# Cross-attention and LoRA experts in float32r: other operand addresses for TensorE, and context means from row sums

## The reference, cut to what matters

```
def attention(h, ctx, mask):                 # h = layernorm(x)
    scores = einsum('bsd,bmd->bsm', h, ctx) / sqrt(1024)
    attn = softmax(where(mask, scores, -1e30))
    return einsum('bsm,bmd->bsd', attn, ctx)   # 0 where nothing is valid
x = x + attention(layernorm(x), ctx, mask)
y = layernorm(x)
base = einsum('btd,od->bto', y, weight)        # 1024 x 1024
logits = einsum('btd,ed->bte', y, router_w)    # 8 experts, the best 2 are used
w_dense = top-2 of softmax(logits), normalised, else 0
Ax = einsum('nd,erd->ner', y, lora_A)          # rank 16 each, 128 columns in all
out = x + base + 2 * einsum('ner,ne,eor->no', Ax, w_dense, lora_B)
```

## Time and profile before

| | before |
|---|---|
| median of three runs | 1052.81 us |
| the profiled execution | 1052.97 us |
| its span | 1051.1 us |
| TensorE matmuls busy | 1042.2 us (99%) |
| VectorE busy | 832.1 us (79%) |
| ScalarE busy | 478.1 us (45%) |
| GpSimd busy | 143.3 us (14%) |

### The profile page before, as it was taken

The page is one execution under the profiler, slowest core; times in us unless marked ns, Lnnn a source line. Parts: engine busy times, 40 slices in busy tenths (PEclk is TensorE's granted clock), DMA queues, the critical chain, the costliest instruction groups (busy, mean ns, idle before and its releaser), DMA issues.

```text
span 1051.1 us, 18389 instructions
## 1 busy us (share of the span) xinstructions
PE 1042.2 (99%) x5849; PEld 1016.9 (97%) x5849; DVE 832.1 (79%) x2230; ACT 478.1 (45%) x930; POOL 143.3 (14%) x278
## 2 busy tenths in 40 slices
PE   7999999999999999999999999999999999999998
PEld 7999999999999999999999999999999999999998
DVE  6988887888777987878877888878888778788763
ACT  7754544445434544444444345344444444443420
POOL 3210111111111111111111111111111111111100
PEclk9999999999999999999999999999999999999999
DMA  8555555654456555575545655455654565554431
GB/s 304 198 168 131 134 153 169 164 155 115 146 160 180 143 132 127 148 200 133 153 116 148 185 150 150 135 132 168 166 151 138 120 171 153 153 149 114 114 78 55
DMA packets 156095, 156.61 MB, mean 149 GB/s; under 512 B 93968, under 2 KB 128912, under 8 KB 156048
## 3 DMA queue, kind: packets, MB, share of 16 engines
q1 hardware_dynamic: 155184, 154.63, 54.0%
q10 hardware_dynamic: 864, 1.45, 0.4%
HBM read 78.74 MB, written 33.55 MB: 107 GB/s over the span
## 4 chain that ended last, share of the span: by engine, by line
PE 96%; DVE 2%; DMA 1%; POOL 0%; issue 0%; ACT 0%; ACTq 0%; DVEq 0%; POOLq 0%
PE base_ps L1106 28%; PE base_ps L1108 28%; PE base_ps L1107 28%; PE s_ps L1133 5%; PE ro_ps L1177 3%; PE ro_ps L1178 3%; DMA xT_raw<-in_xT 1%; DVE w_lo L337 0%; DVE x_first L896 0%; DVE stats L902 0%; DVE xT_parts L815 0%; POOL w_lo L337 0%; PE h_ps L1113 0%; POOL rstd L489 0%; PE base_ps L1150 0%
## 5 line engine op out<-in xcount | busy, mean ns | idle before, releaser
L1106 PE MATMUL base_ps<-w_hi,xT_hi 128*128 128x388 f32 x1512 | 513.9, 340 | 0.0
L1108 PE MATMUL base_ps<-w_hi,xT_lo 128*128 128x388 f32 x1512 | 512.5, 339 | 0.0
L1107 PE MATMUL base_ps<-w_lo,xT_hi 128*128 128x388 f32 x1512 | 511.4, 338 | 0.0
L1107 PEld LDWEIGHTS base_ps<-w_lo,xT_hi 128*128 128x128 f32 x1512 | 284.8, 188 | 2.7
L1106 PEld LDWEIGHTS base_ps<-w_hi,xT_hi 128*128 128x128 f32 x1512 | 284.0, 188 | 2.7
L1108 PEld LDWEIGHTS base_ps<-w_hi,xT_lo 128*128 128x128 f32 x1512 | 284.3, 188 | 0.0
L493 POOL TENSOR_TENSOR rstd<-var_eps,neg_half 128x1 f32<-128x1 f32 x64 | 61.4, 959 | 571.6 <-DVE var_eps L909 571.6
L918 DVE STREAM_TRANSPOSE x2T<-xq 128x512 f32<-128x512 f32 x122 | 121.2, 1069 | 5.1 <-DMA xq<-xn 4.9
L614 ACT CAST xT_hi<-x2T 128x512 fp32r<-128x512 f32 x122 | 69.7, 618 | 79.5 <-DVE x2T L918 79.5
L933 DVE MAX8 top<-base_ps 128x8 f32<-128x8 f32 x64 | 11.1, 174 | 91.7 <-PE base_ps L1108 91.7
L608 ACT ACTIVATE xn<-w_raw,shift,rstd 128x1024 f32<-128x1024 f32 x32 | 39.9, 1246 | 96.5 <-POOL shift L496 96.5
(11 more groups left out here) (131 smaller groups left out, 1342.8 us busy)
## 6 DMA issues: line engine op xcount, KB each, us to landing
xT_raw<-in_xT SPq DMA_DIRECT2D x62, 512.0 KB, 5.3
xq<-xn SPq DMA_DIRECT2D x244, 128.0 KB, 3.6
w_raw<-in_x SPq DMA_DIRECT2D x32, 512.0 KB, 3.5
out<-x_first SPq DMA_DIRECT2D x32, 512.0 KB, 2.7
out<-w_raw SPq DMA_DIRECT2D x31, 512.0 KB, 2.7
x_first<-in_x SPq DMA_DIRECT2D x30, 512.0 KB, 3.5
h<-w_raw SPq DMA_DIRECT2D x248, 16.0 KB, 1.9
w_raw<-w_raw SPq DMA_DIRECT2D x236, 16.0 KB, 2.7
```

Of the source, the lines that this page charges most:

```text
L1106: pe.matmul(out_, a_hi, w_h, start=start, stop=False, skip_group_check=again)
L1107: pe.matmul(out_, a_hi, w_l, start=False, stop=False, skip_group_check=again)
L1108: return pe.matmul(out_, a_lo, w_h, start=False, stop=stop, skip_group_check=again)
```

## The change

The column groups become 392, 384 and 384, and the output columns 256, 384 and 384. The two groups of 384 now stand first in the row, so they begin at bytes 0 and 1536 and the group of 392 at byte 3072; the rows are padded to 1168 columns, 4672 bytes. The total of columns stays 1160. The tiles of one or a few columns are allocated last, so every operand of TensorE in the loop begins on a multiple of 64 bytes.

```
-    SIDE = WC // 6 * 2
+    SIDE = WC // 48 * 16
     W0 = O - 2 * SIDE
-    GROUPS = [(0, W0 + LR), (W0 + LR, SIDE), (W0 + LR + SIDE, SIDE)]
+    WP = -(-WC // 16) * 16
+    GROUPS = [(2 * SIDE, W0 + LR), (0, SIDE), (SIDE, SIDE)]
...
-        w_hi = sb("w_hi", [P, C, WC], f32r)
-        w_lo = sb("w_lo", [P, C, WC], f32r)
+        w_hi = sb("w_hi", [P, C, WP], f32r)
+        w_lo = sb("w_lo", [P, C, WP], f32r)
...
+        row_sums = sb("row_sums", [P, P])
...
-        any_valid = sb("any_valid", [P, 1])
```

```
+                if j == 3 and exists((b, TPB)):
+                    sp.wait_ge(row_sum_stored, b * 16 + 16)
+                    sp.dma_start(row_sums[:, :], ctx_rows.rearrange("q o -> o q").to_broadcast([P, P]))\
+                      .then_inc(row_sums_loaded, 16)
                 store(tile)
...
+                if j == TPB - 5 and exists((b, TPB)):
+                    act.wait_ge(row_sum_done, b + 1)
+                    act.dma_start(ctx_rows, row_sum[:, :]).then_inc(row_sum_stored, 16)
+                if j == TPB - 4 and exists((b, TPB)):
+                    ctxT_high(b + 1)
...
+            def ctx_row_sum(b):
+                dve.wait_ge(ctx_loaded, b * 16 + 16)
+                dve.tensor_reduce(out=row_sum[:, :], in_=ctx_raw[:, 0:D], axis=AX.X, op=ALU.add).then_inc(row_sum_done, 1)
+
             def ctx_centre(b):
-                dve.wait_ge(ctx_mean_done, b + 1)
-                dve.tensor_tensor(ctxT_centred[:, :, :], ctxT_raw[:, :, :],
+                dve.wait_ge(ctxT_loaded, b * 16 + 16)
+                dve.wait_ge(row_sums_loaded, b * 16)
+                for j in range(2):
+                    keys = ctxT_raw[:, :, j * QP:(j + 1) * QP]
+                    sums = row_sums[:, :].rearrange("p (r j) -> p j r", j=Q)[:, j]
+                    dve.scalar_tensor_tensor(out=keys, in0=sums.unsqueeze(1).to_broadcast([P, C, QP]), scalar=-1.0 / D,
+                                             in1=keys, op0=ALU.mult, op1=ALU.add).then_inc(ctx_centred, 1)
...
                 base(tile, 0, range(C))
-                if j == TPB - 4 and exists((b, TPB)):
-                    ctx_mean(b + 1)
                 base(tile, 1, range(HC))
```

More of the change, by code:

```diff
@@ L33, in xattn_lora_moe_kernel @@
     out: bass.AP,
+    ctx_rows: bass.AP,
 ):
@@ L132, in xattn_lora_moe_kernel @@
         ctxT_raw = sb("ctxT_raw", [P, C, M])
-        ctxT_centred = sb("ctxT_centred", [P, C, M])
         ctx_sum = sb("ctx_sum", [P, M])
+        row_sums = sb("row_sums", [P, P])
         mask_f = sb("mask_f", [P, M])
         mask_bias = sb("mask_bias", [P, M])
-        any_valid = sb("any_valid", [P, 1])
         x_first = sb("x_first", [P, XF, D])
@@ L152, in xattn_lora_moe_kernel @@
         one_dth = sb("one_dth", [P, P])
+        s_part = sb("s_part", [P, M])
+        s_all = sb("s_all", [P, M])
+        e_all = sb("e_all", [P, M])
+        e_split = sb("e_split", [P, 2 * M], f32r)
+        eT = sb("eT", [P, P], f32r)
+        h = sb("h", [P, ER])
+        hT_hi = sb("hT_hi", [P, P], f32r)
+        hT_lo = sb("hT_lo", [P, P], f32r)
+        row_sum = sb("row_sum", [P, 1])
+        any_valid = sb("any_valid", [P, 1])
         iota8 = sb("iota8", [P, E])
@@ L167, in xattn_lora_moe_kernel @@
         shift2 = sb("shift2", [P, 1])
-        s_part = sb("s_part", [P, M])
-        s_all = sb("s_all", [P, M])
         neg_max = sb("neg_max", [P, 1])
-        e_all = sb("e_all", [P, M])
-        e_split = sb("e_split", [P, 2 * M], f32r)
         e_sum = sb("e_sum", [P, 1])
@@ L175, in xattn_lora_moe_kernel @@
         e_scale = sb("e_scale", [P, 1])
-        eT = sb("eT", [P, P], f32r)
         top8 = sb("top8", [P, 8])
@@ L184, in xattn_lora_moe_kernel @@
         w_dense = sb("w_dense", [P, E])
-        h = sb("h", [P, ER])
-        hT_hi = sb("hT_hi", [P, P], f32r)
-        hT_lo = sb("hT_lo", [P, P], f32r)
         x_rest = [w_raw[0], w_raw[1], w_raw[1], w_raw[1]]
@@ L278, in xattn_lora_moe_kernel @@
         ctx_mean_done = sem("ctx_mean_done")
+        row_sum_done = sem("row_sum_done")
+        row_sum_stored = sem("row_sum_stored")
+        row_sums_loaded = sem("row_sums_loaded")
         ctx_centred = sem("ctx_centred")
@@ L453, in step @@
                     load_ctx(b + 1)
-                    sp.wait_ge(ctx_centred, b + 1)
+                    sp.wait_ge(ctxT_split, b + 1)
                     load_ctxT(b + 1)
@@ L532, in ctxT_high @@
             def ctxT_high(b):
-                act.wait_ge(ctx_centred, b + 1)
-                act.copy(ctxT[:, :, 0:M], ctxT_centred[:, :, :]).then_inc(ctxT_hi_done, 1)
+                act.wait_ge(ctx_centred, b * 2 + 2)
+                act.copy(ctxT[:, :, 0:M], ctxT_raw[:, :, :]).then_inc(ctxT_hi_done, 1)
             def ctx_high(b):
@@ L671, in step @@
                 gate_exp(tile)
-                if j == TPB - 4 and exists((b, TPB)):
-                    ctxT_high(b + 1)
                 if turned_on_pe(nxt2, 5):
@@ L770, in mask, with first_ctx_sum, first_ctx_centre @@
                 dve.reduce_max(any_valid[:, :], mask_f[:, :], AX.X).then_inc(mask_step, 1)
[L772 to L775, removed]
+            def first_ctx_sum():
+                dve.wait_ge(ctxT_loaded, 16)
+                dve.wait_ge(ctxT_rest_loaded, 16)
                 dve.tensor_reduce(out=ctx_sum[:, :], in_=ctxT_raw[:, :, :].rearrange("p c m -> p m c"), axis=AX.X,
                                   op=ALU.add).then_inc(ctx_sum_done, 1)
+            def ctx_row_sum(b):
+                dve.wait_ge(ctx_loaded, b * 16 + 16)
+                dve.tensor_reduce(out=row_sum[:, :], in_=ctx_raw[:, 0:D], axis=AX.X, op=ALU.add).then_inc(row_sum_done, 1)
             def ctx_centre(b):
-                dve.wait_ge(ctx_mean_done, b + 1)
-                dve.tensor_tensor(ctxT_centred[:, :, :], ctxT_raw[:, :, :],
+                dve.wait_ge(ctxT_loaded, b * 16 + 16)
[5 more added lines that the diff above has]
+                                             in1=keys, op0=ALU.mult, op1=ALU.add).then_inc(ctx_centred, 1)
+            def first_ctx_centre():
+                dve.wait_ge(ctx_mean_done, 1)
+                dve.tensor_tensor(ctxT_raw[:, :, :], ctxT_raw[:, :, :],
                                   h_ps[:, P:P + M].unsqueeze(1).to_broadcast([P, C, M]),
-                                  ALU.subtract).then_inc(ctx_centred, 1)
+                                  ALU.subtract).then_inc(ctx_centred, 2)
             def ctxT_low(b):
                 dve.wait_ge(ctxT_hi_done, b + 1)
-                dve.tensor_tensor(ctxT[:, :, M:2 * M], ctxT_centred[:, :, :], ctxT[:, :, 0:M].bitcast(f32),
+                dve.tensor_tensor(ctxT[:, :, M:2 * M], ctxT_raw[:, :, :], ctxT[:, :, 0:M].bitcast(f32),
                                   ALU.subtract).then_inc(ctxT_split, 1)
@@ L1006, in step @@
                 h_transposes(tile)
-                if j == TPB - 4 and exists((b, TPB)):
-                    ctx_centre(b + 1)
                 if j == TPB - 3 and exists((b, TPB)):
@@ L1013, in step @@
                         x2_transposes(nxt, i)
+                if j == TPB - 5 and exists((b, TPB)):
+                    ctx_row_sum(b + 1)
+                if j == TPB - 4 and exists((b, TPB)):
+                    ctx_centre(b + 1)
                 if j % 2 == 1 and exists(after(tile, 3)):
@@ L1023, in step @@
                     x2T_low(nxt)
-                if j == TPB - 5 and exists((b, TPB)):
-                    ctx_sum_chunks(b + 1)
                 if j == TPB - 4 and exists((b, TPB)):
@@ L1038, in _ @@
             dve.wait_ge(constants_ready, CONSTANTS)
-            ctx_sum_chunks(0)
-            ctx_centre(0)
+            first_ctx_sum()
+            first_ctx_centre()
             first_xT_low(0, 0)
@@ L1108, in three, with first_ctx_mean @@
                 return pe.matmul(out_, a_lo, w_h, start=False, stop=stop, skip_group_check=again)
-            def ctx_mean(b):
-                pe.wait_ge(ctx_sum_done, b + 1)
+            def first_ctx_mean():
+                pe.wait_ge(ctx_sum_done, 1)
                 pe.matmul(h_ps[:, P:P + M], one_dth[:, :], ctx_sum[:, :], start=True, stop=True).then_inc(ctx_mean_done, 1)
@@ L1251, in _ @@
             pe.wait_ge(constants_ready, CONSTANTS)
-            ctx_mean(0)
+            first_ctx_mean()
             warm(5)
@@ L1358 @@
     O = weight.shape[0]
-    w0 = O - 2 * ((O + E * R + E) // 6 * 2)
+    w0 = O - 2 * ((O + E * R + E) // 48 * 16)
     mask_words = np.ascontiguousarray(mask).view(np.float32)[:, None, :].repeat(P, axis=1)
@@ L1367 @@
         "ctxT": np.stack([by_contraction(rows) for rows in ctx]),
-        "wT": by_quadrants(np.concatenate([weight[:w0], lora_a.reshape(E * R, D), router, weight[w0:]])),
+        "wT": by_quadrants(np.concatenate([weight[w0:], weight[:w0], lora_a.reshape(E * R, D), router])),
         "bT": by_blocks(lora_b.transpose(0, 2, 1).reshape(E * R, O)),
@@ L1374 @@
     out = nc.dram_tensor("out", (B * S // P, P, O), mb.dt.float32, kind="ExternalOutput").ap()
```

(3 more changed lines are left out.)

## The result

The changed kernel takes 1060.16 us, the median of four runs (1059.16 to 1060.67), against 1052.68 us before: 1.0072 times as long, 95% interval 1.006 to 1.0084. It is slower by 7.5 us where 3.9 us less were forecast. Its profiled execution took 1060.59 us, with a span of 1058.8 us.

A forecast was written before the change was run, and what follows sets the result against it. TensorE was taken as the bound, its matmuls busy 99% of the span. The terms -1.6 (mean), -1.4 (column groups) and -0.9 (pair scores) sum to -3.9 us: 1049.1 profiled, median 1048.9, range 1037 to 1054.2.

The forecast's parts named there:

- the way through DRAM: Store of the row sums by ScalarE, then load by SyncE and two subtractions on VectorE: claimed to cost nothing.
- The room: Slack before TensorE takes the next step's `xT_lo`: 1.7 us, against at most 1.2 us of lateness in VectorE's readout addition.
- rival C: Load of the sums lands late in step 4, TensorE waits 1.25 us in 7 batches: +8.8 us, 1057.7; chance 0.10.
- The mean: Step with the mean's matmul is 0.23 us longer; it falls away in 7 batches: -1.6 us, the firmest term.
- The addresses: Operands of TensorE's matmuls in the loop moved to aligned places: -1.4 us for column groups, -0.9 us for pair scores.
- A: TensorE's matmuls: addresses do nothing, only the mean's matmul goes, -1.6 us, 1051.2; chance 0.26.
- D: TensorE's column groups: the 392 columns cost and the 384 give nothing, -1.6 + 2.9 us, 1054.1; chance 0.08.
- The count of 64-byte pieces: Moving operands in `base` and `lora_second`: one cycle per 64-byte piece touched, 73 pieces instead of 75, -1.4 us.
- Pair scores: Their matmuls touch 8 pieces of 64 bytes instead of 9: 3.5 to 4 ns each in 29 steps, -0.9 us.
- Rival B: `base` and `lora_second` gain only with both operands on multiples of 64: 1030 to 1041.4 us, middle 1036; chance 0.18.
- The stationary operand's place seems worth nothing: Matmuls of 386 columns take 176.7 ns in `lora_second`, stationary operand on a multiple of 64, as in `base`, off one.
- VectorE's sum: New row sum of 1024 elements, 1.1 to 2.2 us, stands where VectorE waited 1.12 us: claimed to cost nothing.

The follow-up runs named there:

- the fastest kernel: The changed kernel with the sums transposed before the store and SyncE's load of them moved ahead of the exchange of the activations: 1047.66 us, ratio 0.9954.

## Why the prediction was wrong

**The step that failed** is "the way through DRAM", where the store got "11 us for the store". I priced it only by when it would be ready, and left out what it does to the DMAs beside it. Its neighbours in time are the four DMAs of `s_exchange`, whose landing releases VectorE. In place of 0 it costs 9 us in the changed kernel (the run without it; 10.4 against the run with turned sums) and 12.3 us in the kernel before (the run with it added). The nearest row for its landing was 1.9 us for 16 KB in pieces of 128 bytes; 4-byte pieces took 7.3.

**The room was misread too**, in the same step. I measured it to `xT_lo`, 1.7 us. But `hT_lo` stands ahead of it in VectorE's order and `lora_second` needs it earlier. Before, in step (1, 4):

```profile
233.07 0.27 DVE L972 TENSOR_TENSOR hT_lo<-h,hT_hi 128x128 fp32r<-128x128 f32 x1
```

```profile
234.86 0.28 PE L1106 MATMUL base_ps<-b_hi,hT_hi 128*128 128x252 f32 x1
```

That is 234.86 - 233.34 = 1.5 us, 1.3 when the mean's 0.23 is gone. Against it stood a load that landed after 3.0 to 3.9 us and subtractions of 1.15 us. With the sums turned, so without the store's harm, the readout's addition began 0.8 to 1.5 us later in the step than before, and step (b, 4) was longer than 15.01 us in just the four batches where it was 1.3 or more. "At most 1.2" of lateness was optimistic, and "the least margin of all" was right. This is rival C, and the load's place cost 2.1 us where C said 8.8. C's sign was right and its total (1057.7) came near the result by luck, because the store, which it does not have, made up the rest; it had 0.10.

**The mean** was right: step (b, 4) takes 15.27 us where the addresses alone were changed, and 15.01 in the fastest kernel, as the other even steps; 0.25 us in 7 batches, 1.8 us.

**The addresses** came out at -2.45 us where -2.3 were forecast, but not by the terms that were given; that the totals are so near is in part luck. A gain of that size, clear of the noise, rules out rivals A and D. The count of 64-byte pieces gave the column groups -1.4 us, and alone they cost +2.2; the tile order was given -0.9 and alone gave -0.3. Together, a tile's `base` takes 12.69 us for 12.72 before (24 matmuls of 392 columns 4.26, of 384 columns 4.20 and 4.22; forecast 4.29 and 4.20). The third group took about 0.03 us more than the second before and takes 0.02 more with all on multiples of 64, so that difference does not come only from its place 8 bytes past a multiple of 16. Pair scores lengthen a step by 1.85 us for 1.90, which is -1.4 us in 29 steps where -0.9 was forecast. The readout, given nothing, got slower: 0.94 us for 0.91 in even steps. Rival B said that it takes both operands on multiples of 64. For whole steps that is how it came out, with a price several times too high, but `lora_second` and the last group of `base` do not follow it. "The stationary operand's place seems worth nothing" was read where the weights were not all on 64: there the group of 388 takes 4.25 and 4.26 us with it off and on. With the weights on 64 the group of 392 takes 4.30 and 4.26. Which reads collide, or whether any do, stays open.

**VectorE's sum** cost nothing that shows, as said: 1.19 us in a gap of 1.12, and the fastest kernel, which has it, keeps its steps (b, 4) at 15.01 us.

The sum from the measured parts is 1052.4 - 2.45 - 1.8 + 9 to 10.4 (store) + 2.1 (load's place), 1059.3 to 1060.7, and the result is 1060.16. That it closes proves little, since 9 and 10.4 are differences to that result. With the 12.3 us of the kernel before it would be 1062.6, too much. Why the store costs less beside the new addresses is not shown. Its harm varies from batch to batch: the steps (b, 4) of the changed kernel are 0.8 to 2.6 us longer than those of the fastest.

## What to carry to other kernels

A small DMA is to be priced by its pieces and by its neighbours, not by its bytes: turn a column into rows before it is stored. Put the load of a value that is long ready ahead of the queue's waits, not behind them. Room for a late instruction is measured to the first of all the consumers behind it in the engine's order.

## What the runs showed of the hardware that was not expected

A store of 128 pieces of 4 bytes from SBUF to DRAM takes 7.3 to 7.6 us to complete (medians of two kernels), against 2.4 us for 64-byte and 2.5 us for 512-byte pieces. Nearly all of that is behind the last piece: 5.2 to 6.7 us, against 0.3 to 1.0 for the larger ones. While it is open, DMAs issued from another queue complete late (5 us for 1.9): 3.3 to 4.3 us behind their last piece in the changed kernel, against 0.3 beside the stores of larger pieces. The Trainium skill ("DMA: Bandwidth & Descriptors", section "Anatomy of one DMA — SWDGE (gpsimd) path") puts most of the fixed 2 us down to the receipt of the last write. It describes another path than this queue's; the idle engines here agree with a wait for a receipt, and no run shows the receipt itself. TensorE's distance between float32r matmuls depends on where its operands lie, by some nanoseconds and not by one operand alone: the same even step takes 15.01 us with the operands of `base` both on multiples of 64, 15.03 with neither, 15.05 with the stationary one alone and 15.09 with the weights alone, on the average over the loop.
